# Who issues the small transfers of an attention kernel's partial sums: the sync engine's queue or ScalarE's

## What is computed

```python
ada = silu(c) @ Wada + bada
shift_msa, scale_msa, gate_msa, shift_mlp, scale_mlp, gate_mlp = split(ada, 6)
h = ln(x) * (1 + scale_msa) + shift_msa
q, k, v = h @ Wq + bq, h @ Wk + bk, h @ Wv + bv          # (2, 2048, 16, 32)
A = softmax(q k^T / sqrt(32))
x = x + gate_msa * ((A v) @ Wo + bo)
h2 = ln(x) * (1 + scale_mlp) + shift_mlp
out = x + gate_mlp * (gelu(h2 @ W1 + b1) @ W2 + b2)
```

## Time and profile before

| | us |
|---|---|
| median of 3 runs | 3004.51 (2996.43 to 3007.48) |
| the profiled execution | 2994.86 |
| its span in the profile | 2993.0 |

### The profile page before, as it was taken

How to read it: one execution, slowest core, us unless ns; L and a number is a source line. 1 busy time by engine, 2 the same in 40 slices (tenths; PEclk the granted TensorE clock), 3 DMA queues, 4 the chain that set the end, 5 groups by cost and what they waited for, 6 DMA issues and landing times.

```text
span 2993.0 us, 49503 instructions
## 1 busy us (share of the span) xinstructions
PE 2499.4 (84%) x19544; PEld 1370.3 (46%) x19544; DVE 1755.8 (59%) x2878; ACT 1422.0 (48%) x2622; POOL 1504.9 (50%) x706
## 2 busy tenths in 40 slices
PE   7998747788877778887787888878888878899998
PEld 5787513333333333333333333333333334788887
DVE  5444536566665656666565666656666642565663
ACT  3323025556655556665555666555666654222211
POOL 0000025667666666756566665666676663433230
PEclk9999868889998988899888999989899988999999
DMA  7655321111112111111211111121111211221210
GB/s 255 203 177 169 104 88 60 51 45 45 51 55 59 55 49 45 45 52 55 56 58 47 45 45 50 56 60 57 46 45 49 61 57 38 66 85 56 81 60 29
DMA packets 204947, 210.33 MB, mean 70 GB/s; under 512 B 112384, under 2 KB 145152, under 8 KB 195328
## 3 DMA queue, kind: packets, MB, share of 16 engines
q1 hardware_dynamic: 204016, 207.40, 22.7%
q10 hardware_dynamic: 720, 0.02, 0.0%
HBM read 146.30 MB, written 60.82 MB: 69 GB/s over the span
## 4 chain that ended last, share of the span: by engine, by line
PE 57%; SPq 30%; DMA 6%; ACT 3%; DVE 2%; issue 2%; POOL 0%; ACTq 0%; POOLq 0%; DVEq 0%
SPq L506 20%; PE ps L1242 16%; PE ps L1373 12%; SPq L489 8%; PE ps L1482 6%; PE ps L1339 6%; PE ps L1351 5%; PE ps L1364 4%; PE ps L1353 3%; PE ps L1355 2%; PE ps L1360 2%; DMA partial_sums<-work 2%; DMA q_lo<-work 1%; ACT work L842 1%; SPq L482 1%
## 5 line engine op out<-in xcount | busy, mean ns | idle before, releaser
L715 POOL TENSOR_TENSOR work<-work 128x1024 f32<-128x1024 f32 x576 | 1354.4, 2384 | 855.8 <-ACT work L861 610.0
L1068 DVE TENSOR_REDUCE part_max<-ps 128x1 f32<-128x512 f32 x1984 | 1242.5, 683 | 724.0 <-PE ps L1339 723.3
L861 ACT ACTIVATE work<-ps 128x512 f32<-128x512 f32 x2048 | 1061.9, 602 | 421.8 <-PE ps L1360 413.1
L1339 PE MATMUL ps<-acts_r 32*128 32x512 f32 x1344 | 423.7, 519 | 263.3 <-ACT work L842 239.1
L1373 PE MATMUL ps<-work 128*32 128x512 f32 x4096 | 614.7, 676 | 0.0
L1242 PE MATMUL ps<-acts_r,weights_r 128*128 128x512 f32 x1536 | 382.9, 399 | 4.9 <-DVE acts_r L988 3.9
L1339 PEld LDWEIGHTS ps<-acts_r 32*128 32x128 f32 x1344 | 184.3, 201 | 373.2 <-ACT work L842 266.7
L842 ACT ACTIVATE work<-ps 128x512 f32<-128x512 f32 x224 | 134.0, 598 | 456.9 <-DMA partial_sums<-work 400.2
L1351 PE MATMUL ps<-acts_r 32*128 32x512 f32 x1408 | 308.5, 494 | 33.2 <-DVE work L1001 22.6
L1242 PEld LDWEIGHTS ps<-acts_r,weights_r 128*128 128x128 f32 x1536 | 293.2, 192 | 70.0 <-issue 6.8
L1351 PEld LDWEIGHTS ps<-acts_r 32*128 32x128 f32 x1408 | 144.0, 200 | 374.7 <-DVE part_max L1068 195.8
(11 more groups left out here) (88 smaller groups left out, 2387.6 us busy)
## 6 DMA issues: line engine op xcount, KB each, us to landing
acts_r<-k_hi SPq DMA_DIRECT2D x32, 1024.0 KB
acts_r<-k_lo SPq DMA_DIRECT2D x32, 1024.0 KB
work<-in_x SPq DMA_DIRECT2D x16, 1024.0 KB, 5.4
q_hi<-work SPq DMA_DIRECT2D x32, 256.0 KB, 2.6
q_lo<-work SPq DMA_DIRECT2D x32, 256.0 KB, 3.3
k_hi<-work SPq DMA_DIRECT2D x32, 256.0 KB, 2.6
k_lo<-work SPq DMA_DIRECT2D x32, 256.0 KB, 3.2
v_rows<-work SPq DMA_DIRECT2D x32, 256.0 KB, 2.0
```

The source lines that it names most:

```text
L715: nc.gpsimd.tensor_tensor(psum_acc[:, at], first, prob[:, t % RING, at], ALU.add).then_inc(add_ok, 1)
L861: nc.scalar.activation(prob[:, t % RING, j * CH:(j + 1) * CH], ps[:, bank, :], ACT.Exp, scale=SCALE).then_inc(exp_ok, 1)
L1068: nc.vector.tensor_reduce(part_max[:, r * TT + q // NQ, q % NQ:q % NQ + 1], ps[:, bank, :], AX.X, ALU.max).then_inc(a_max, 1)
L1339: nc.tensor.matmul(ps[:, use[0], :], q_hi[u][at, q // NQ * P:(q // NQ + 1) * P], k_hi[u][at, q % NQ * CH:(q % NQ + 1) * CH], start=True, s ...
```

## The change

The store of each partial sum goes from SP's program to ACT's. ACT issues it on its own DMA queue right behind the copy, after waiting for the copy's own semaphore. SP's program loses all seven stores of a head and the waits on `sums_ok` with them; the wait for the last one of a buffer before the end part is written out. Buffers, banks, PE's, DVE's and POOL's programs stay as they were.

```diff
             def head(g):
-                def sums_of(steps):
-                    for t in steps:
-                        store_sums(g if t > 1 else g - 1, USES[g][t]["sums"])
                 sp.wait_ge(b_mm, g * FILLS)
                 if g + 2 < G:
                     load_hi(g + 2, (g + 2) % HI_BUF)
-                sums_of((0,))
                 sp.wait_ge(pv_mm, START + g * NT)
                 load_lo(g + 1, (g + 1) % TWO)
                 load_v(g + 1, (g + 1) % TWO)
                 store_head(g - 1, (g - 1) % TWO)
-                sums_of(range(1, 5))
                 load_sums(g - 1)
-                sums_of(range(5, 9))
                 store_rec(g - 1)
-                sums_of(range(9, NT - 1))
                 put_max(g + 1, (g + 1) % TWO)
-                sums_of((NT - 1,))
...
+            sp.wait_ge(sums_out[1], 16 * sums_before(SUMS_END, 1))
...
             def take_sums(g, uses):
...
                     nc.scalar.activation(sums[b], ps[:, bank, :], ACT.Copy).then_inc(sums_ok, 1)
+                    act.wait_ge(sums_ok, n)
+                    act.dma_start(sums_dram[g * ND + d:g * ND + d + 1, :].rearrange("o (r q) -> (o r) q", q=CH),
+                                  sums[b][0:P:DH, :]).then_inc(sums_out[b], 16)
```

More of the change, by code:

```diff
@@ L507, in store_head @@
                                  o_st[u][j * DH:(j + 1) * DH, :].rearrange("d (r q) -> d r q", q=P)).then_inc(o_out[u], 16)
[L509 to L515, removed]
             def load_sums(g):
@@ L573, in _ @@
                 if k >= 2:
-                    store_sums(0, USES[0][k]["sums"])
                     sp.wait_ge(late_hi, k - 1)
@@ L583, in _ @@
                     load_lo(1, 1)
-            for t in range(len(late), NT - 1):
-                store_sums(0, USES[0][t]["sums"])
             put_max(1, 1)
-            store_sums(0, USES[0][NT - 1]["sums"])
             for g in range(1, G - 2):
@@ L623, in _ @@
             load_first_oT(0)
-            uses = USES[G - 1]
-            store_sums(G - 2, uses[0]["sums"])
             store_head(G - 2, 0)
-            store_sums(G - 2, uses[1]["sums"])
+            sp.wait_ge(sums_out[1], 16 * sums_before(SUMS_END, 1))
             heads_stored(G - 1)
@@ L633, in _ @@
             load_sums(G - 2)
-            for t in range(2, STEP_RECIP + 1):
-                store_sums(G - 1, uses[t]["sums"])
             store_rec(G - 2)
-            for t in range(STEP_RECIP + 1, NT):
-                store_sums(G - 1, uses[t]["sums"])
-            store_sums(G - 1, USES_END[:1])
             sp.wait_ge(pv_mm, START + G * NT)
@@ L644, in _ @@
             store_head(G - 1, 1)
-            store_sums(G - 1, USES_END[1:])
             heads_stored(G)
```

## The result

The changed kernel took 2812.2 us in the median of three runs (2809.13 to 2815.22), 0.9365 of the time before (95% interval 0.9332 to 0.9398). That is 192 us less; 234 less was forecast, as 2770. The profiled execution took 2812.2 us.

A forecast was written before the change was run, and what follows sets the result against it. PE, 84% busy, was bound with two stops a head at ACT's partial-sum copies. A 65.07 us head becomes 49.6 + 5.8 + 1.5 + 0.5 = 57.4, saving 234 us in all: 2770 us, own range 2700 to 2850, 8-in-10 range 2690 to 3210.

The forecast's parts named there:

- The two stops go: ACT's partial-sum copies D and E no longer wait for earlier transfers to land; gives back up to 15.5 us a head.
- The wait that comes in its place: DVE, at its denominators, waits 5.8 us a head for the seven sums that SP fetches back; PE stands behind it.
- a dense head: A head without stops, summed from the distances between partial-sum copies: 49.6 us, against 65.07 before the change.
- SP's head start: SP issues q and k's high parts 3.1 us earlier and the sums' fetch gains 1.7; sums back at copy A + 33.7.
- SP's chain keeps its length: SP's loads of q, k and v and its outputs, ahead of the sums' fetch, take as long as before.
- The wait and the clock: DVE's wait at its denominators, 5.8 us a head, and PE's slow clock behind that stop, 1.5 us.
- ACT's 0.5: Cost on ACT of issuing the seven partial-sum transfers, mostly covered by its wait for PE: 0.5 us a head.
- The sum: A head takes 57.4 us, 7.7 less; 222 us over 29 heads plus 12 for head 30, 234 in all.
- The rival in which ACT is held: ACT's issues wait while SP is held in its own; 3110 to 3295 us, middle 3200; chance 0.30.
- The rival in which ACT's transfers land late: ACT's transfers wait for SP's earlier loads; copy C stands 8.9 us, a head takes 59.7 us, total 2836; chance 0.12.
- The rival in which DVE does not stand: Transfers finish sooner, so the denominators do not wait; a head is 50.1 us, total 2557; chance 0.08.

The follow-up runs named there:

- Experiments 1 and 2: Denominators at step 12 instead of 8: 1 in the changed kernel, 2543.11 us; 2 in the kernel before, reciprocals' store moved later too, 3006.48 us.
- experiment 5: Changed kernel, SP again waiting for partial-sum copies A and B before the high and low parts, but storing nothing: 2880.53 us, ratio 0.9601.
- experiments 3 and 4: Each q and k load split into four transfers of 32 rows: 3 in the changed kernel, 2502.31 us; 4 in the kernel before, 2499.94 us.

## Why the prediction held, step by step

**The two stops go.** Right: no copy of the changed kernel waited for a transfer but C, 12 times and 9.4 us in all, and never longer than 1.2 us.

**The wait that comes in its place.** Right in kind and place: DVE stands at its denominators, PE behind it, in every head. Experiments 1 and 2 show it from both sides: it is all that is left over a dense head after the change, and nothing before it.

**SP's head start.** Right in kind; experiment 5 shows it one for one. But here is the term that was mis-sized: I had the sums back at A + 33.7 us, 3.1 and 1.7 earlier than before. In the shown head they came at 1539.79 - 1504.36 = A + 35.4, in the mean of 28 heads at A + 35.2. Both parts of the head start are there (q was issued 1.8 us ahead of A, where it was 1.2 behind; the fetch stands 0.1 us behind the outputs' issues, where it was 1.7). The chain between them got longer. In the shown heads it is 34.9 us from q's issue to the end of the outputs', against 1570.76 - 1537.67 = 33.1 before; but heads differ (31.3 to 36.0 before, 31.8 to 38.9 after), and the one that I had read before lay below its mean. The means of 28 heads are 33.6 before and 34.8 after, so 1.2 us longer. "SP's chain keeps its length", which the prediction called its second weakest step, is the step that did not hold. Why is open: in the pair of experiments 1 and 2, with the same two orders of SP's queue, the chain is 34.2 and 34.1 us, so the order alone did not lengthen it there, and no experiment was made to tell what does; part of the 1.2 us can be scatter, as these are single traces.

**The wait and the clock.** 5.8 us forecast, 6.4 measured in the shown head, 6.6 in the mean of all 31. In the shown head C's wait for A made DVE 1 us later, which hid as much of the late sums. From the denominators to the next A it was 1563.62 - 1539.79 = 23.8 us; forecast were 21.7 for the dense part, 1.5 for the slow clock and 0.5 for ACT's issues, 23.7. Of these, ACT's 0.5 was nothing that could be measured, as experiments 3 and 4 show for a dense head, and the clock, if the dense part is taken as forecast, was 2.1. Two small misses cancel here, which is luck.

**The sum.** A head is 59.1 us instead of 57.4. That is 1.7 x 29 = 49 us, of the 51 us by which the forecast was short from one profiled execution to the other (2994.86 - 2812.2 = 183 instead of 234). Between the medians it is 42 short, because the profiled execution before lay 10 us under its median and the one after lies on it.

**The rival in which ACT is held.** It had 0.30, and it is refuted: 87 of ACT's 224 issues lie wholly inside issues of SP's of more than 3 us, and none of the 87 took over 0.50 us; the longest of all 224, at 412.16, took 1.07. SP's longest single issue, 26.7 us, is the first of these four, and an issue of ACT's falls into it:

```profile
613.62 28.17 SPq L506 DMA_DIRECT2D attention_T<-work  x4
...
631.52 0.50 ACTq L815 DMA_DIRECT2D partial_sums<-work  x1
```

What had spoken against the rival, the twelve engines that stood idle while SP was held, pointed the right way: it fits a wait for room in SP's own queue, though no run tests that by itself. The Trainium skill, Perfetto Trace Analysis, section on the hardware-issued DMA instruction, says that the block that generates descriptors is locked for exclusive use until all are generated. If so, SP did not have the lock in the stretches in which ACT's issues went through; the page does not say when in such a hold it is taken.

**The rival in which ACT's transfers land late.** A's 7.7 us in the shown head are over four times the 1.7 of an undisturbed one, but A's transfer did not wait for the high parts issued ahead of it: C would have stood 8.9 us and stood 0.97. The packets from q's issue to C's copy, 1502.5 to 1512.6, say the same; q1 is SP's queue and q10 ACT's:

```profile
q1 hardware_dynamic: 182, 0.67, 22.3%
q10 hardware_dynamic: 8, 0.01, 0.3%
```

The eight packets on q10 are A's transfer. It was through when 0.67 of the 1.31 MB of q's and k's high parts had moved. A transfer on ACT's queue shares the engines with SP's and does not line up behind them.

**The rival in which DVE does not stand** is refuted as well: the chain was longer than thought, not shorter. It told the price of what could still be had, 2557; experiment 1 took it, at 2543.

## What to carry to other kernels

When a stop is removed, ask what else was late and had been covered by it: here the fetch of the sums was late all along, at the same place in the queue, and took back 9 of the 15 us a head that the change freed. Before moving the small transfers away from the large ones, look at why the large ones take long: a DMA share of 0.26 that does not move is a transfer that runs on a quarter of the engines, and its shape, 32 rows instead of 4 copies, was worth 17.0% of the time (with some 29 us ahead of the first head), where moving the issuer was worth 6.35% and, once the shape was mended, nothing that could be measured. A load that is moved to be out of someone's way needs its own deadline looked up in the code first.

## What the runs showed of the hardware

- ACT's issue of a transfer was not held while SP's was: 87 issues of ACT's inside holds of SP's of up to 26.7 us, none over 0.50 us (median of all 224: 0.48).
- A transfer of 8 KB issued by ACT while SP's 1 MB load was under way landed after 7.7 us; an undisturbed one of 4 KB took 1.7.
- Loads of q and k whose first dimension is 4 held the DMA share at 0.26 and 75 GB/s; the same bytes as four transfers of 32 rows ran at a share of 0.86 and 204 GB/s.
